# Attention rounds taken in twos on TensorE: scores and maxima of two rounds, then row sums and value products of two rounds

## The chip, the cores and the metric

The kernel runs on one core of a Trainium2 chip. The metric is the device time of one execution in microseconds (us), the median of several runs. The engines named below are TensorE (PE in the rows; PEld is its weight load, which can overlap matmuls), VectorE (DVE), ScalarE (ACT), GpSimd (POOL) and SyncE (SP, which here only issues DMAs).

## What is computed

A layer norm, then attention with ALiBi bias and a causal mask, plus a top-1 mixture of experts on the same normed input. Shapes: x is 2 x 2048 x 512, 16 heads of 32, 8 experts.

```python
xn = layernorm(x)
q, k, v = split(xn @ W_qkv)                       # to heads: (2, 16, 2048, 32)
attn = softmax(q @ k.T / sqrt(32) + alibi + causal_mask)
y = (attn @ v) @ W_o
idx = argmax(softmax(xn @ wg)); gate = max(softmax(xn @ wg))
out = x + y + gate * (xn @ W[idx].T + b[idx])
```

## The kernel before

The program has four parts one after another: projections and routing (`project_and_route`), attention (`attend`), the experts (`run_experts`) and the sum (`combine`). The change is in `attend` alone.

**Groups and rounds.** `attend` works through 8 groups `g` of 4 heads (`HG`). The queries of a group are cut in 4 chunks of 512 (`QC`), the keys in 16 blocks of 128. A round is one chunk and one key block; with the causal mask a chunk `c` needs 4(c+1) blocks, so a group has `NR` = 40 rounds (`ROUNDS`): 4, 8, 12 and 16 in the four chunks. The last 4 rounds of a chunk lie on the diagonal: their tiles are 512, 384, 256 and 128 columns wide and get an extra small matmul that adds the mask (L1129). Group 0 is written out with a plan of its own (`PLAN_FIRST`), groups 1 to 6 use `PLAN_MID` (2 to 5 of them in a hardware loop of two groups per turn), group 7 uses `PLAN_LAST`.

**What TensorE does in a round.** Four scores (`score_unit`, L1126, one per head, full 128-column array, into one of `S_BANKS` = 3 PSUM banks in turn); ScalarE takes the exponential of each bank into `probs` (L1061) and so frees it. Between the scores lie units of the row maxima (`max_unit`, L1091, with a mask matmul L1094 on the diagonal; `M_BANKS` = 3 banks), which VectorE reduces (L975). These maxima belong to rounds far ahead, four units per round in the middle groups (5 to 6 in group 0, none in the last 26 rounds of group 7). Then come the value products of the round before (`value_products`, L1170): four matmuls of 32 columns each, one per head, side by side in the array. The row sums (`row_sums`) have the same 32-column form: on a diagonal round straight from `probs` (L1161); elsewhere two rounds (a pair, `PAIR_OF`) are first added by GpSimd (L959) and TensorE sums the pair (L1137) two rounds later. A matmul of the row sums or value products is shown as two in the trace (x8 for four heads). Below, the 32-column work is called tile work and a run of it a tile block.

**The order.** It is written out by hand: in round r the scores and maxima go unit by unit; the row sums of round r-1 stand in the middle of them (at `hh == HG // 2`, L1191), the value products of round r-1 at the end (L1195).

**The end of a chunk.** Both accumulators lie in one pair of PSUM banks (`acc_ps`). After the last round of a chunk ScalarE copies them out (`leave`, L1043), VectorE inverts the denominators in four quarters (L1010), one each at the end of its next rounds, and GpSimd multiplies (L936); SyncE stores the result (L851). The copy waits until the store of the chunk two before has landed (`y_stored`, L1042), since it overwrites that buffer. `LEAVE_AT`, `INVERT_AT` and `Y_BEFORE_PAIR` say at which round or pair each of these steps stands.

**SyncE's queue** goes in a fixed order: the rows of maxima of later chunks (L842, L846), the load of the next group's queries, keys and values (L813 to L834), which waits for the value products of the group before, and the stores. A store that is issued behind the group's load lands after it. In group 0 the load of group 1 also waits until GpSimd has scattered the normed rows to their expert slots; that scatter stands in GpSimd's queue behind its first additions and the first chunk's multiplication.

Of the kernel before, what the change touches and what calls it, by code (L numbers as in the profile page):

```python
# [26 lines left out]
HG = P // DH  # L27
# [3 lines left out]
QC = S // CH  # L31
# [17 lines left out]
ROUNDS = [(c, jb) for c in range(QC) for jb in range(TPC * (c + 1))]  # L49
NR = len(ROUNDS)  # L50
# [10 lines left out]
NPAIR = len(PAIR_OF) // 2  # L61
PAIR_LAST = {p: r for r, p in PAIR_OF.items()}
LAST_ROUND = [max(r for r, (cc, _) in enumerate(ROUNDS) if cc == c) for c in range(QC)]
# [3 lines left out]
UNIT, FOLD, TURN, SPLIT = "unit", "fold", "turn", "split"  # L67
# [69 lines left out]
def plan_of(g, last):  # L137
# [3 lines left out]
    if isinstance(g, int) and g == 0:  # L141
# [3 lines left out]

LEAVE_AT = {(LAST_ROUND[c] + 1) % NR: ((LAST_ROUND[c] + 1) // NR, c) for c in range(QC)}
QUARTERS = 4
INVERT_AT = {(LAST_ROUND[c] + 2 + k) % NR: ((LAST_ROUND[c] + 2 + k) // NR, c, k)  # L150
             for c in range(QC) for k in range(QUARTERS)}

Y_BEFORE_PAIR = {min([p for p in range(NPAIR) if PAIR_LAST[p] > (LAST_ROUND[c] + 2 + QUARTERS) % NR] or [NPAIR]):
                 ((LAST_ROUND[c] + 2 + QUARTERS) // NR, c) for c in range(QC)}


class Memory:
# [583 lines left out]
def attend(nc, m):  # L741
# [6 lines left out]
    with ExitStack() as c:  # L748
# [24 lines left out]
        max_rows_loaded = [sem("max_rows_loaded0"), sem("max_rows_loaded1")]  # L773
# [11 lines left out]
        MAX_ROWS = 16 * (1 + 2 * HG)  # L785
# [19 lines left out]
        with nc.Block() as block:  # L805
# [268 lines left out]
            def _(pe):  # L1074
# [22 lines left out]
                def maxima(events, banks, g, half, taken):  # L1097

                    for dg, kind, n in events:
                        if (dg, kind, n) == (1, UNIT, 0):  # L1100

                            pe.wait_ge(aug_loaded[1 - half], AUG * ((g + 1) // 2 + 1))
                        if isinstance(g, int) and g == 0 and (dg, kind, n) == (0, UNIT, OF_CHUNK[1][0]):
                            pe.wait_ge(first_loaded[1], AUG)
                        if isinstance(g, int) and g == 0 and (dg, kind, n) == (0, UNIT, OF_CHUNK[QC - 1][0]):

                            pe.wait_ge(aug_loaded[0], AUG)
                        bank, earlier = banks[dg, kind, n]
                        bank_free(earlier, g, taken)
                        if kind == UNIT:  # L1110
                            max_unit((half + dg) % 2, n, bank)
                        else:
                            pe.wait_ge(neg_done, (g + dg) * QC + n + 1)
                            nc.tensor.transpose(max_ps[:, bank, 0:P], neg_max[:], m.ident[:]).then_inc(max_turned, 1)
# [33 lines left out]
                def has_row_sums(r):  # L1148
                    return r not in PAIR_OF or r - 2 in PAIR_LAST.values()

                def row_sums(g, r, exps, adds):

                    cc, jb = ROUNDS[r]
                    off = max(0, jb - TPC * cc) * P
                    probs_of(g, r, exps)

                    if r - 2 in PAIR_LAST.values():
                        pair_product(PAIR_OF[r - 2], ROUNDS[r - 2] == (cc, 1), adds)
                    if r not in PAIR_OF:
                        for hh in range(HG):  # L1160
                            nc.tensor.matmul(den_ps[hh * DH:(hh + 1) * DH, off:CH], m.ones[:],  # L1161
                                             probs[:, r % P_SLOTS, hh, off:CH], start=jb == 0, stop=r == LAST_ROUND[cc])
# [12 lines left out]
                def step(g, half, first, last):  # L1175
                    if first:
                        pe.wait_ge(first_loaded[2], AUG)
                    pe.wait_ge(v_loaded[half], 16 * (g // 2 + 1))
                    exps, adds = base(pe, g, NSU), base(pe, g, NPAIR * HG)
                    taken = base(pe, g, NMU), None if last else base(pe, g + 1, NMU)  # L1180
                    plan, banks = plan_of(g, last)
                    for r in range(NR + 1):
                        events = [e for e in plan[r] if e[1] in (UNIT, TURN)] if r < NR else []
                        if r < NR and ROUNDS[r][1] == 0:

                            cc = ROUNDS[r][0]
                            pe.wait_ge(max_rows_loaded[cc % 2], MAX_ROWS * (g * (QC // 2) + cc // 2 + 1))
                        for hh in range(HG):
                            if r < NR:
                                score_unit(half, r, hh, first, exps)  # L1190
                            if r and hh == HG // 2 and has_row_sums(r - 1):  # L1191
                                row_sums(g, r - 1, exps, adds)
                            maxima(events[len(events) * hh // HG:len(events) * (hh + 1) // HG], banks, g, half, taken)
                        if r:
                            value_products(g, half, r - 1, exps)  # L1195

                pe.wait_ge(first_loaded[0], AUG)
                events = [e for e in PLAN_BEFORE[0] if e[1] in (UNIT, TURN)]
# [317 lines left out]
```

## Time and profile before

| | us |
|---|---|
| median of 3 runs | 1939.15 |
| lowest, highest | 1935.37, 1945.24 |
| span of the profiled execution | 1937.1 |
| TensorE busy | 1789.7 (92%) |
| VectorE busy | 1131.4 (58%) |
| ScalarE busy | 913.7 (47%) |
| GpSimd busy | 665.3 (34%) |
| TensorE, scores L1126, 1280 matmuls | 531.1 |
| TensorE, maxima L1091, 1280 matmuls | 523.6 |
| TensorE, value products L1170, 2560 matmuls | 308.6 |

The span runs from the first to the last instruction; the median of the runs is 2.05 us above it. Attention takes the time from about 340 to 1668 us. The last group's copy of its last chunk begins at 1667.9; those of groups 0 to 6 at 592.5, 750.5, 906.4, 1071.1, 1225.2, 1381.3 and 1539.3. In a table of windows each engine has its busy time, and PEclk is the granted TensorE clock as a share of full speed (1.00 is 2.4 GHz, 0.50 is 1.2 GHz).

### The profile page before, as it was taken

The numbers are of one execution on the slowest core, as the hardware profiler recorded it, in microseconds if no ns is written. First come the engines' busy times: TensorE is split into PE (matmuls) and PEld (weight loads), VectorE is DVE, ScalarE is ACT, GpSimd is POOL, SyncE is SP. The second block draws the span as 40 slices with busy tenths as digits, with TensorE's granted clock in tenths as the row PEclk, the third lists the DMA queues.
The fourth block names the chain that finished last, engine by engine and source line by source line (L and its number), as shares of the span: only waits on it lengthen the run. The fifth ranks groups of instructions, "written<-read, shape, count | busy, mean of one in ns | idle before, by whom it ended". The sixth has DMA issues, their size and how long they took to land. (4 is left out here: it accounts for less than half of the span.)

```text
span 1937.1 us, 31890 instructions
## 1 busy us (share of the span) xinstructions
PE 1789.7 (92%) x10482; PEld 1023.6 (53%) x10483; DVE 1131.4 (58%) x2001; ACT 913.7 (47%) x1575; POOL 665.3 (34%) x665
## 2 busy tenths in 40 slices
PE   5999999589699999999999999999999999789798
PEld 4777777344344444444444444444444443478687
DVE  5433334577487577666665667767766670344366
ACT  3222222055356566565565566656656567621211
POOL 6000000067152452442444246245244346211260
PEclk9999999588899899999899899999989999899999
DMA  6667744959508205502700900730450230244496
GB/s 229 220 216 261 266 168 147 163 204 252 64 7 145 32 7 104 68 14 58 114 8 9 169 8 7 139 39 7 99 72 8 76 116 12 104 152 163 145 390 240
DMA packets 102350, 227.81 MB, mean 118 GB/s; under 512 B 9832, under 2 KB 27240, under 8 KB 96648
## 3 DMA queue, kind: packets, MB, share of 16 engines
q1 hardware_dynamic: 87648, 176.20, 36.3%
q0 software_dynamic: 14560, 49.75, 7.0%
q8 instruction: 84, 1.38, 0.3%
q14 instruction: 58, 0.48, 0.1%
HBM read 128.47 MB, written 96.93 MB: 116 GB/s over the span
## 5 line engine op out<-in xcount | busy, mean ns | idle before, releaser
L1061 ACT ACTIVATE probs_sb<-score_ps,bias 128x512 f32<-128x512 f32 (+3 forms) x1280 | 733.1, 624 | 506.2 <-PE score_ps L1129 303.7
L975 DVE TENSOR_REDUCE part_max<-max_ps 128x1 f32<-128x512 f32 (+3 forms) x1280 | 722.0, 603 | 394.5 <-PE max_ps L1091 203.0
L959 POOL TENSOR_TENSOR pair_sum<-probs_sb 128x512 f32<-128x512 f32 x384 | 479.8, 1281 | 592.5 <-ACT probs_sb L1061 592.3
L1126 PE MATMUL score_ps<-q_aug,k_aug 100*128 100x512 f32 (+3 forms) x1280 | 531.1, 422 | 42.3 <-ACT probs_sb L1061 24.4
L1091 PE MATMUL max_ps<-k_aug,q_aug 98*128 98x512 f32 (+3 forms) x1280 | 523.6, 421 | 40.1 <-DMA q_aug<-q_rows_d 33.4
L1126 PEld LDWEIGHTS score_ps<-q_aug,k_aug 100*128 100x128 f32 x1280 | 251.3, 197 | 305.9 <-ACT probs_sb L1061 231.5
L1091 PEld LDWEIGHTS max_ps<-k_aug,q_aug 98*128 98x128 f32 x1280 | 260.2, 204 | 181.7 <-DVE part_max L975 104.7
L1170 PE MATMUL acc_ps<-probs_sb,v_sb 128*32 128x512 f32 (+3 forms) x2560 | 308.6, 555 | 0.0
L1010 DVE RECIPROCAL acc_sb<-acc_sb 128x128 f32<-128x128 f32 x128 | 119.6, 939 | 74.0 <-ACT acc_sb L1043 74.0
L618 DVE SCALAR_TENSOR_TENSOR st_lo<-group_ps,st_hi 128x512 fp32r<-128x512 f32 x64 | 44.3, 692 | 139.1 <-ACT st_hi L665 138.4
L1094 PE MATMUL max_ps<-mask_qk,ident_bf 128*128 128x128 bf16 x512 | 124.3, 243 | 0.0
L1129 PE MATMUL score_ps<-mask_kq,ident_bf 128*128 128x128 bf16 x512 | 120.0, 235 | 0.0
L665 ACT ACTIVATE st_hi<-group_ps 128x512 fp32r<-128x512 f32 x64 | 38.3, 598 | 143.0 <-PE group_ps L728 124.2
L728 PE MATMUL group_ps<-xT_hi,w_hi 128*128 128x512 f32 x256 | 102.7, 401 | 0.0
L1137 PE MATMUL acc_ps<-pair_sum,ones 128*32 128x512 f32 x768 | 102.3, 605 | 0.0
L728 PE MATMUL group_ps<-xT_lo,w_hi 128*128 128x512 f32 x256 | 101.9, 398 | 0.0
L728 PE MATMUL group_ps<-xT_hi,w_lo 128*128 128x512 f32 x256 | 101.7, 397 | 0.0
L1161 PE MATMUL acc_ps<-probs_sb,ones 128*32 128x512 f32 (+3 forms) x1024 | 97.3, 452 | 1.2 <-ACT acc_sb L1043 1.2
L1094 PEld LDWEIGHTS max_ps<-mask_qk,ident_bf 128*128 128x128 bf16 x512 | 52.7, 103 | 75.1 <-issue 56.9
L1129 PEld LDWEIGHTS score_ps<-mask_kq,ident_bf 128*128 128x128 bf16 x512 | 50.6, 99 | 69.1 <-issue 48.6
L1170 PEld LDWEIGHTS acc_ps<-probs_sb,v_sb 128*32 128x32 f32 x2560 | 51.5, 109 | 63.7 <-issue 39.8
L466 POOL DMA_DIRECT2D slot_x_d<-zero_f x20 | 14.2, 715 | 172.2 <-PE group_ps L728 172.2
(177 smaller groups left out, 1684.5 us busy)
## 6 DMA issues: line engine op xcount, KB each, us to landing
k_aug<-k_hi_d SPq DMA_DIRECT2D x14, 1024.0 KB
q_aug<-q_hi_d SPq DMA_DIRECT2D x14, 1024.0 KB
slot_x_d<-zero_f POOLq DMA_DIRECT2D x20, 512.0 KB, 7.1
rows<-slot_x_d SPq DMA_DIRECT2D x40, 256.0 KB, 2.6
slot_y_d<-y_rows POOLq DMA_DIRECT2D x39, 256.0 KB, 2.5
xn_d<-xn SPq DMA_DIRECT2D x8, 1024.0 KB, 9.9
q_hi_d<-st_hi SPq DMA_DIRECT2D x32, 256.0 KB, 7.7
q_lo_d<-st_lo SPq DMA_DIRECT2D x32, 256.0 KB, 7.6
```

The costliest lines, as they stand in the source:

```text
L728: last = nc.tensor.matmul(group_ps[:, n % BANKS], lhs, rhs, start=(k == 0 and p == 0), stop=(k == KC - 1 and p == 2))
L959: nc.gpsimd.tensor_tensor(pair_sum[:, p % 2, hh], probs[:, s0, hh], probs[:, s1, hh], ALU.add).then_inc(pair_added, 1)
L975: nc.vector.tensor_reduce(part_max[:, hh * QT + i, kc:kc + 1], max_ps[:, bank, 0:w], AX.X, ALU.max).then_inc(max_taken, 1)
L1010: nc.vector.reciprocal(quarter, quarter).then_inc(inverted, 1)
L1061: nc.scalar.activation(probs[:, r % P_SLOTS, hh, off:CH], score_ps[:, (r * HG + hh) % S_BANKS, off:CH], ACT.Exp, bias=bias[:, half, hh * Q ...
L1091: last = nc.tensor.matmul(max_ps[:, bank, 0:w], q_aug[0:ROW_MAX, half, hh, i * P:(i + 1) * P], k_aug[0:ROW_MAX, half, hh, kc * CH:kc * CH ...
L1094: last = nc.tensor.matmul(max_ps[:, bank, w - P:w], m.ident_bf[:], m.mask_qk[:], start=False, stop=True)
L1126: last = nc.tensor.matmul(score_ps[:, u % S_BANKS, off:CH], k_aug[0:ROWS, half, hh, jb * P:(jb + 1) * P], q_aug[0:ROWS, half, hh, cc * CH ...
L1129: last = nc.tensor.matmul(score_ps[:, u % S_BANKS, off:off + P], m.ident_bf[:], m.mask_kq[:], start=False, stop=True)
L1137: last = nc.tensor.matmul(den_ps[hh * DH:(hh + 1) * DH, :], m.ones[:], pair_sum[:, p % 2, hh], start=start, stop=False)
L1161: nc.tensor.matmul(den_ps[hh * DH:(hh + 1) * DH, off:CH], m.ones[:], probs[:, r % P_SLOTS, hh, off:CH], start=jb == 0, stop=r == LAST_ROUN ...
L1170: last = nc.tensor.matmul(y_ps[hh * DH:(hh + 1) * DH, off:CH], v_sb[:, half, jb, hh * DH:(hh + 1) * DH], probs[:, r % P_SLOTS, hh, off:CH] ...
```

## The change

The loop over rounds becomes a loop over pairs of rounds (r0, r0+1). For each, TensorE runs the eight scores and their maxima in a row, then the row sums and value products of the two rounds r0-2 and r0-1. Nothing is added to or taken from the matmuls. As the value products of a chunk's last round now come one round later, the copy, the reciprocals and the multiplication are moved one round later too.

```diff
-LEAVE_AT = {(LAST_ROUND[c] + 1) % NR: ((LAST_ROUND[c] + 1) // NR, c) for c in range(QC)}
+LEAVE_AT = {(LAST_ROUND[c] + 2) % NR: ((LAST_ROUND[c] + 2) // NR, c) for c in range(QC)}
 QUARTERS = 4
-INVERT_AT = {(LAST_ROUND[c] + 2 + k) % NR: ((LAST_ROUND[c] + 2 + k) // NR, c, k)
+INVERT_AT = {(LAST_ROUND[c] + 3 + k) % NR: ((LAST_ROUND[c] + 3 + k) // NR, c, k)
              for c in range(QC) for k in range(QUARTERS)}
...
-                    for r in range(NR + 1):
-                        events = [e for e in plan[r] if e[1] in (UNIT, TURN)] if r < NR else []
...
-                        for hh in range(HG):
-                            if r < NR:
+                    for r0 in range(0, NR + 2, 2):
+                        for r in (r0, r0 + 1) if r0 < NR else ():
+                            events = [e for e in plan[r] if e[1] in (UNIT, TURN)]
...
+                            for hh in range(HG):
                                 score_unit(half, r, hh, first, exps)
-                            if r and hh == HG // 2 and has_row_sums(r - 1):
-                                row_sums(g, r - 1, exps, adds)
-                            maxima(events[len(events) * hh // HG:len(events) * (hh + 1) // HG], banks, g, half, taken)
-                        if r:
-                            value_products(g, half, r - 1, exps)
+                                maxima(events[len(events) * hh // HG:len(events) * (hh + 1) // HG], banks, g, half, taken)
+                        for r in (r0 - 2, r0 - 1) if r0 else ():
+                            if has_row_sums(r):
+                                row_sums(g, r, exps, adds)
+                            value_products(g, half, r, exps)
```

`Y_BEFORE_PAIR` changes in the same way (+2 to +3), and gives the same pairs as before.

TensorE in the fourth chunk of group 1, a pair of full-width rounds. Before, one round with the pair's row sums in its middle:

```order
L1126 MATMUL score_ps<-q_aug,k_aug 128x512
L1091 MATMUL max_ps<-k_aug,q_aug 128x128
L1094 MATMUL max_ps<-mask_qk,ident_bf 128x128
L1126 MATMUL score_ps<-q_aug,k_aug 128x512
L1137 MATMUL acc_ps<-pair_sum,ones 32x512 x4
L1091 MATMUL max_ps<-k_aug,q_aug 128x128
L1094 MATMUL max_ps<-mask_qk,ident_bf 128x128
L1126 MATMUL score_ps<-q_aug,k_aug 128x512
L1091 MATMUL max_ps<-k_aug,q_aug 128x128
L1094 MATMUL max_ps<-mask_qk,ident_bf 128x128
L1170 MATMUL acc_ps<-probs_sb,v_sb 32x512 x4
L1126 MATMUL score_ps<-q_aug,k_aug 128x512
```

The change, the end of one pair's units and the start of the next:

```order
L1126 MATMUL score_ps<-q_aug,k_aug 128x512
L1091 MATMUL max_ps<-k_aug,q_aug 128x256
L1094 MATMUL max_ps<-mask_qk,ident_bf 128x128
L1170 MATMUL acc_ps<-probs_sb,v_sb 32x512 x4
L1137 MATMUL acc_ps<-pair_sum,ones 32x512 x4
L1170 MATMUL acc_ps<-probs_sb,v_sb 32x512 x4
L1126 MATMUL score_ps<-q_aug,k_aug 128x512
L1091 MATMUL max_ps<-k_aug,q_aug 128x512
```

Three separate tile blocks in a pair of rounds have become one.

TensorE in the last group, where no maxima are left. Before:

```order
L1126 MATMUL score_ps<-q_aug,k_aug 128x512 x3
L1137 MATMUL acc_ps<-pair_sum,ones 32x512 x4
L1126 MATMUL score_ps<-q_aug,k_aug 128x512
L1170 MATMUL acc_ps<-probs_sb,v_sb 32x512 x4
L1126 MATMUL score_ps<-q_aug,k_aug 128x512 x4
L1170 MATMUL acc_ps<-probs_sb,v_sb 32x512 x4
```

The change:

```order
L1126 MATMUL score_ps<-q_aug,k_aug 128x512 x8
L1170 MATMUL acc_ps<-probs_sb,v_sb 32x512 x4
L1137 MATMUL acc_ps<-pair_sum,ones 32x512 x4
L1170 MATMUL acc_ps<-probs_sb,v_sb 32x512 x4
L1126 MATMUL score_ps<-q_aug,k_aug 128x512 x8
```

Eight scores now follow each other with nothing between them, against three banks.

ScalarE in a middle group at the passage from the second chunk to the third, with the semaphores that each instruction waits for (`scored`: TensorE's score; `pv_done`: the value products; `y_stored1`: the store two chunks back). Before:

```order
L1061 ACTIVATE probs_sb<-score_ps,bias 128x512 [waits scored,pv_done]
L1061 ACTIVATE probs_sb<-score_ps,bias 128x512 [waits scored] x3
L1043 ACTIVATE acc_sb<-acc_ps 128x1024 [waits y_stored1,pv_done]
L1061 ACTIVATE probs_sb<-score_ps,bias 128x512 [waits scored,pv_done]
L1061 ACTIVATE probs_sb<-score_ps,bias 128x512 [waits scored] x3
```

The change:

```order
L1061 ACTIVATE probs_sb<-score_ps,bias 128x512 [waits scored,pv_done]
L1061 ACTIVATE probs_sb<-score_ps,bias 128x512 [waits scored] x3
L1061 ACTIVATE probs_sb<-score_ps,bias 128x512 [waits scored,pv_done]
L1061 ACTIVATE probs_sb<-score_ps,bias 128x512 [waits scored] x3
L1043 ACTIVATE acc_sb<-acc_ps 128x1024 [waits y_stored1,pv_done]
L1061 ACTIVATE probs_sb<-score_ps,bias 128x512 [waits scored,pv_done]
```

The copy stands one round of four exponentials later.

## Rows read from the trace of the kernel before

**Rows 1.** Windows of middle and last groups: length, busy per engine, PEclk, DMA share, GB/s.

```profile
1100.00:1300.00 200.00, 194.04 (x1289) 90.00 (x1285) 138.01 (x245) 123.61 (x217) 85.72 (x70) 0.98 0.32 53
1600.00:1700.00 100.00, 82.31 (x568) 39.62 (x561) 26.37 (x40) 67.09 (x122) 42.81 (x36) 0.94 0.15 56
```

**Rows 2.** Timeline, TensorE, middle group: start, us, engine, line, operation, count.

```profile
704.18 0.50 PE L1126 MATMUL score_ps<-q_aug,k_aug 100*128 100x512 f32 x1
...
709.94 0.40 PE L1126 MATMUL score_ps<-q_aug,k_aug 100*128 100x512 f32 x1
...
710.17 0.39 PE L1091 MATMUL max_ps<-k_aug,q_aug 98*128 98x512 f32 x1
...
710.49 1.06 PE L1170 MATMUL acc_ps<-probs_sb,v_sb 128*32 128x512 f32 x8
...
711.49 0.50 PE L1126 MATMUL score_ps<-q_aug,k_aug 100*128 100x512 f32 x1
...
711.82 0.28 PE L1091 MATMUL max_ps<-k_aug,q_aug 98*128 98x256 f32 x1
...
740.37 1.07 PE L1137 MATMUL acc_ps<-pair_sum,ones 128*32 128x512 f32 x8
741.25 0.83 PE L1161 MATMUL acc_ps<-probs_sb,ones 128*32 128x384 f32 x8
```

**Rows 3.** Timeline, ScalarE and VectorE in the same group; then page row of the reciprocals.

```profile
704.80 2.42 ACT L1061 ACTIVATE probs_sb<-score_ps,bias 128x512 f32<-128x512 f32 x4 [0.96 <-PE score_ps L1126]
...
719.56 2.48 DVE L975 TENSOR_REDUCE part_max<-max_ps 128x1 f32<-128x512 f32 x4 [0.83 <-PE max_ps L1091]
...
L1010 DVE RECIPROCAL acc_sb<-acc_sb 128x128 f32<-128x128 f32 x128 | 119.6, 939 | 74.0 <-ACT acc_sb L1043 74.0
```

**Rows 4.** Last group: timeline of ScalarE and TensorE, then a window, TensorE alone.

```profile
1621.80 2.45 ACT L1061 ACTIVATE probs_sb<-score_ps,bias 128x512 f32<-128x512 f32 x4
...
1622.57 0.50 PE L1126 MATMUL score_ps<-q_aug,k_aug 100*128 100x512 f32 x1 [0.99 <-ACT probs_sb L1061]
1622.99 1.06 PE L1170 MATMUL acc_ps<-probs_sb,v_sb 128*32 128x512 f32 x8
...
1629.51 0.96 PE L1126 MATMUL score_ps<-q_aug,k_aug 100*128 100x512 f32 x3
...
1635.60 0.96 PE L1126 MATMUL score_ps<-q_aug,k_aug 100*128 100x512 f32 x3
...
1640.00:1650.00 10.00, 9.05 (x53) 1.00 0.07 27
```

**Rows 5.** Load, store, copy of a middle group: timeline, a window, waits, then group 4.

```profile
744.05 0.64 SPq L842 DMA_DIRECT2D q_aug<-q_rows_d  x1
...
750.02 0.36 SPq L813 DMA_DIRECT2D k_aug<-k_hi_d  x1
...
747.56 0.47 PE L1126 MATMUL score_ps<-q_aug,k_aug 100*128 100x512 f32 x1
...
797.88 1.02 ACT L1043 ACTIVATE acc_sb<-acc_ps 128x1024 f32<-128x1024 f32 x1 [3.45 <-DMA y_d<-acc_sb]
...
799.54 0.80 PE L1126 MATMUL score_ps<-q_aug,k_aug 100*128 100x512 f32 x1 [3.33 <-ACT probs_sb L1061]
...
800.00:805.00 5.00, 5.00 (x21) 2.20 (x21) 2.74 (x6) 2.61 (x6) 4.52 (x4) 0.54 0.00 0
...
ACT acc_sb L1043 <- DMA y_d<-acc_sb: 19.0, 5, 4.1
...
1065.25 0.38 SPq L813 DMA_DIRECT2D k_aug<-k_hi_d  x1
...
1066.25 0.76 PE L1126 MATMUL score_ps<-q_aug,k_aug 100*128 100x512 f32 x1 [4.43 <-DMA q_aug<-max_lo]
```

**Rows 6.** Group 0: GpSimd's first multiplication; what TensorE waited for, 470 to 510.

```profile
432.32 1.28 POOL L936 TENSOR_TENSOR acc_sb<-acc_sb 128x512 f32<-128x512 f32 x1 [0.18 <-DVE acc_sb L1010]
...
PE max_ps L1091 <- DMA q_aug<-q_rows_d: 15.6, 1, 15.6
```

More of the change, by code:

```diff
@@ L143, in plan_of @@
     return PLAN_MID, BANKS_MID
-LEAVE_AT = {(LAST_ROUND[c] + 1) % NR: ((LAST_ROUND[c] + 1) // NR, c) for c in range(QC)}
+LEAVE_AT = {(LAST_ROUND[c] + 2) % NR: ((LAST_ROUND[c] + 2) // NR, c) for c in range(QC)}
 QUARTERS = 4
-INVERT_AT = {(LAST_ROUND[c] + 2 + k) % NR: ((LAST_ROUND[c] + 2 + k) // NR, c, k)
+INVERT_AT = {(LAST_ROUND[c] + 3 + k) % NR: ((LAST_ROUND[c] + 3 + k) // NR, c, k)
              for c in range(QC) for k in range(QUARTERS)}
-Y_BEFORE_PAIR = {min([p for p in range(NPAIR) if PAIR_LAST[p] > (LAST_ROUND[c] + 2 + QUARTERS) % NR] or [NPAIR]):
-                 ((LAST_ROUND[c] + 2 + QUARTERS) // NR, c) for c in range(QC)}
+Y_BEFORE_PAIR = {min([p for p in range(NPAIR) if PAIR_LAST[p] > (LAST_ROUND[c] + 3 + QUARTERS) % NR] or [NPAIR]):
+                 ((LAST_ROUND[c] + 3 + QUARTERS) // NR, c) for c in range(QC)}
 class Memory:
@@ L1181, in step @@
                     plan, banks = plan_of(g, last)
-                    for r in range(NR + 1):
-                        events = [e for e in plan[r] if e[1] in (UNIT, TURN)] if r < NR else []
-                        if r < NR and ROUNDS[r][1] == 0:
-                            cc = ROUNDS[r][0]
-                            pe.wait_ge(max_rows_loaded[cc % 2], MAX_ROWS * (g * (QC // 2) + cc // 2 + 1))
-                        for hh in range(HG):
-                            if r < NR:
-                                score_unit(half, r, hh, first, exps)
-                            if r and hh == HG // 2 and has_row_sums(r - 1):
-                                row_sums(g, r - 1, exps, adds)
-                            maxima(events[len(events) * hh // HG:len(events) * (hh + 1) // HG], banks, g, half, taken)
-                        if r:
-                            value_products(g, half, r - 1, exps)
+                    for r0 in range(0, NR + 2, 2):
+                        for r in (r0, r0 + 1) if r0 < NR else ():
+                            events = [e for e in plan[r] if e[1] in (UNIT, TURN)]
+                            if ROUNDS[r][1] == 0:
+                                cc = ROUNDS[r][0]
+                                pe.wait_ge(max_rows_loaded[cc % 2], MAX_ROWS * (g * (QC // 2) + cc // 2 + 1))
+                            for hh in range(HG):
+                                score_unit(half, r, hh, first, exps)
+                                maxima(events[len(events) * hh // HG:len(events) * (hh + 1) // HG], banks, g, half, taken)
[3 more added lines that the diff above has]
+                            value_products(g, half, r, exps)
                 pe.wait_ge(first_loaded[0], AUG)
```

## The prediction, made before the changed kernel was run

> **What bounds the kernel now.** I read the windows first, to see which engine is full in which stage. In the middle groups TensorE is busy 194 of 200 us, VectorE 138 and ScalarE 124; in the last group TensorE is busy 82 of 100 us and ScalarE 67 [rows 1]. So seven of eight groups go by TensorE's queue, and the last one by TensorE and ScalarE in turn. A busy share near full says nothing of waste inside it, so the timeline of TensorE came next, read by start times: what a matmul costs is the distance to the next start. Then the waits, for what holds TensorE up at all: in each of five middle groups ScalarE's copy waits for a store, 19.0 us together, and in group 0 TensorE waits 15.6 us once for a load [rows 5, 6].
>
> **What the change removes: switches between full matmuls and tile blocks.** In a steady run the next full matmul starts after 0.23 us (709.94 to 710.17). Before a tile block it takes 0.32 (to 710.49): 0.09 more. A 512-wide block of four heads takes 0.88 us if tile work follows it (740.37 to 741.25), but 1.00 if a full matmul does (710.49 to 711.49): 0.12 more. The first full matmul behind it takes 0.33 instead of 0.23, since its weight load is not hidden: 0.10 more [rows 2]. One tile block between full matmuls so costs 0.09 + 0.12 + 0.10 = 0.31 us of switching. (The Trainium skill, TensorEngine Tiling (Array Packing), section Key Properties, says that a change of tiling mode drains the engine; it gives no price, and the rows agree with 0.31 us.)
>
> How many go: before, a group has 39 blocks at ends of rounds (the last holds rounds 38 and 39) and 24 in the middle of rounds (15 diagonal rounds, and 9 of the 12 pair sums; the other three stand beside diagonal ones). That is 63. After, there are 20 pairs, the last two tile blocks touch, so 19. 44 fewer x 0.31 = **13.6 us per group**, 109 us over eight groups. That is the gross gain, and I do not expect most of it to arrive.
>
> **What it adds: eight units in a row against three banks.** ScalarE takes the first exponential 0.62 us after the first score starts (704.18 to 704.80) and four take 2.42 us, so about 0.58 each [rows 2, 3]. A score may start 0.77 us after the start of the exponential that empties its bank (1621.80 to 1622.57) [rows 4]. The eighth score needs the fifth exponential: 0.62 + 4 x 0.58 + 0.77 = 3.71 us after the first. TensorE itself would be there after 0.33 + 0.23 + 6 x 0.46 = 3.3 to 3.4. So it waits about 0.35, and a held matmul shows its weight load (0.10), which makes 0.45 us per full-width pair. Before, a tile block after at most four scores gave ScalarE that time for nothing. A middle group has 12 such pairs: 5.4 us. In the 8 diagonal pairs the scores are narrower, and VectorE paces instead: four reductions in 2.48 us, 0.60 each, hardly below 3.9 us for the eighth maximum where TensorE's narrower units would need 3.2 to 3.6. I take 0.4 each, 3.2 us. Then the reciprocals, 0.94 us each [rows 3]: before, there was one per round, worked off during the tile blocks. Now 8 of the 20 pairs hold two, the first one between the fourth and the fifth maximum of a run that VectorE already paces, and in four of these ScalarE starts with its copy (1.02 us) [rows 5]. Of the 0.94 I take 0.4 to 0.5 as visible, with the turn of the maxima in the middle of a run: 3.5 us net of what such places cost now. Sum **+12.1 us per middle group**, so nets to -1.5 us, or -9 us for six. The unknown here is the pace: with 0.15 us per pair less or more it is 18 us either way in these six groups, 23 in all.
>
> Nothing else lengthens in between: GpSimd's four additions of a pair (5 us of a 7 us pair) now wait until the sums of two pairs ago are used, some 2 us later than now, and their results are wanted two pairs on. Registers and semaphores are the same in number. I cost these at nothing; the cover is the idle half of GpSimd.
>
> **What it moves: the store that arrives late.** In five middle groups ScalarE waits 3.45 to 4.1 us (19.0 in all) at the copy of the second chunk; TensorE then stands still for 3.3 us, and after that runs at about half clock for some 5 us (0.54 from 800 to 805), 2.3 to 2.7 us lost [rows 5]. A place so costs about 6.3 us, five are 31.5. The store lands 47.9 us after SyncE starts to issue the next group's load (750.02 to 797.88), because it lies behind that load; the load itself starts 2.5 us after the group's first score (747.56), because SyncE is still issuing rows of maxima from 744.05 on, for about 5.6 us. So it lands at 50.3 us of the group. After the change the turn of those maxima has the second half of a run of eight and the tile work of four rounds between it and the group's end, over 7 us in place of 4.7, so the load starts with the group and the store lands at about 48. The copy comes one round of scores later: before, the value products of round 11 were through at 46.7; less 15 switches (4.7 us), plus round 13's units (1.9) and about 5 us of the new waits, they end at 48 to 49. So the wait goes or nearly so, and with it the drop of the clock. Group 4 supports this: there the load started 1.0 us before the first score (1065.25, 1066.25), and its copy did not wait [rows 5]. I take **-31.5 us**; if only the timing of the load were unchanged, it would be 0 to -10.
>
> **Group 0.** Its first part is bound by GpSimd's queue: the multiplication of chunk 0 follows the last reciprocal with hardly a wait (0.18 us), and behind it stand the rest of the scatter, the load of group 1 and TensorE's wait of 15.6 us for it [rows 6]. The last reciprocal now comes a round later, behind 5 or 6 more reductions (3.3 us and the turn): +4 us, straight to the end of that wait. What TensorE itself loses before it is absorbed by the 15.6. Behind the load 19 rounds with 5.6 maxima each follow, where VectorE needs 11 x 0.60 + reciprocals per pair and stood closest to the limit: +0.5 us per pair, 5 us. Together **+9 us**.
>
> **The last group.** Its first 14 rounds are as in a middle group, 0. Then no maxima stand between the scores: a pair takes 3.71 to the eighth score, 0.42 from a held score to the tile block (1622.57 to 1622.99), and 0.88 + 0.88 + 1.00 of tile work: 6.89 us, against 6.09 now (1629.51 to 1635.60) [rows 2, 4]. Nine full pairs at +0.8 and four diagonal ones at about +0.5: **+9 us**.
>
> **Sum.** -9 - 31.5 + 9 + 9 = -22.5 us on the span of 1937.1, which gives 1914.6; with the 2.05 us between that span and the median, **1917 us**.
>
> **The rivals.**
> 1. The pace hides: VectorE and ScalarE start each run empty, and if the waits come to about 0.2 us per pair instead of 0.45, some 36 us more stay: 1917 - 36 = 1881. For it: both are a third or more idle in the middle groups. Against: 3.71 is a chain of measured distances.
> 2. The late store stays late. If the load of the next group starts no sooner after the first score, the copy meets the same 50.3 us, and rounds that go faster only wait longer: the 31.5 us are not gained, 1948. It decides at the first 12 rounds: the value products of round 11 have to end after the store lands, with a margin of a few tenths by my sum.
> 3. Slower by the pace: a bank's hand-over costs more when two engines hold TensorE in turns, because each held matmul shows its load. At 0.2 us more per pair, 156 pairs give +31: 1948; at 0.3, 1964. For it speaks the last group, which waits for ScalarE at nearly each round already. This is slower from +0.08 us per pair on top of mine being wrong elsewhere, or from +0.2 alone.
> 4. The clock. Now TensorE waits some tenths in many rounds of the last group, and the granted clock stays at 1.00 [rows 4]; it falls only behind waits of 3 us and more. A wait in each run that did lower it, say one half-clock stretch of 2.3 us per chunk, would give 32 x 2.3 = +74: 1991. (The Trainium skill, TensorE: Matmul & The Clock Gate, section A second HAM failure mode: psum-queue depth-cycling, tells of a kernel that cycles through PSUM banks and whose short idle times between groups of matmuls make the clock swing. The trace disagrees so far as waits of some tenths go.)
> 5. That the change does not do what it says can be left out: the order of instructions shows the merged blocks.
>
> **Chances.** Mine 0.50, with a range of its own of 1900 to 1932; rival 1 0.16; rival 2 0.14; rival 3 0.16; rival 4 0.03; 0.01 for the rest. For 8 in 10, the range leaves out half of rival 1's far side and rival 4 with the far half of rival 3: 1885 to 1953. About 0.5% (9.7 us) is what a measurement can tell from no change: faster means below 1929.5, slower above 1948.8. Faster: 0.44 of mine and rival 1, 0.60; same: the rest of mine and half of rivals 2 and 3, 0.19; slower 0.21.
>
> **What would show it.** Right: 19 tile blocks per group, pairs of about 7.0 to 7.1 us in the fourth chunk of the middle groups instead of 7.3 (704.18 to 711.49), no wait of the copy at L1043 for a store, no clock below 0.9 behind it, a last group some 9 us longer than its 128.6, and a copy of group 0's last chunk some 9 us later. Wrong: pairs of 6.7 us (rival 1), a wait of 3 us or more at L1043 with the half-clock stretch behind it (rival 2), pairs of 7.3 or more (rival 3), PEclk under 0.9 all through a group (rival 4).

## The result: 2.7% faster, more than twice the gain that was forecast

The changed kernel takes **1890.15 us** (median of 4 runs, 1886.1 to 1890.46) against 1937.34 for the kernel before, measured beside it: a ratio of 0.973 (95% interval 0.971 to 0.976), 47 us less. The forecast was 1917 with a range of 1885 to 1953: the direction was right and the time lies in the range, but the likeliest case forecast 22 us less (1939.15 to 1917), and its own range of 1900 to 1932 was missed. The largest term that failed is the pace, +12.1 us per middle group. The profiled execution spans 1884.5 us against 1937.1.

The account by groups comes from ScalarE's copy of each group's last chunk (L1043 in ScalarE's timeline). After the change it begins at 603.75, 748.30, 892.73, 1045.10, 1193.26, 1337.59, 1481.93 and 1614.46 us.

| | before | after | difference | forecast |
|---|---|---|---|---|
| start to group 0's last copy | 592.5 | 603.8 | +11.3 | +9 |
| groups 1 to 6 | 946.8 | 878.2 | -68.6 | -40.5 |
| group 7 | 128.6 | 132.5 | +3.9 | +9 |
| to the end of the span | 269.2 | 270.0 | +0.8 | 0 |
| span | 1937.1 | 1884.5 | -52.6 | -22.5 |

So the question of this study is the 28 us in the middle groups. In every kernel below group 3 takes 5 to 9 us more than its undisturbed neighbours 1, 2, 5 and 6. Between groups 3 and 4 the hardware loop turns; TensorE stands still there for 4.4 us in the changed kernel and then runs at a granted clock of 0.50 from 1036 to 1056 us. An order can be compared best in the undisturbed groups; the expectations give their length as that of the middle groups (151.0, 144.35), the results below give the mean of all six.

The window of the profile of after that answers to the first of [rows 1] (length, then busy time of TensorE, its weight load, VectorE, ScalarE and GpSimd, then PEclk, DMA share, GB/s):

```profile
1100.00:1300.00 200.00, 196.88 (x1375) 103.30 (x1377) 145.00 (x264) 128.88 (x235) 94.27 (x77) 1.00 0.26 47
```

TensorE is as full as before and does 1375 matmul records in the time of 1289; its clock is 1.00 instead of 0.98. A busy share would have shown nothing of the gain.

TensorE's timeline in the fourth chunk of group 5, the end of one pair and of the next, to be held against [rows 2]:

```profile
1291.28 1.07 PE L1170 MATMUL acc_ps<-probs_sb,v_sb 128*32 128x512 f32 x8
1292.16 1.04 PE L1137 MATMUL acc_ps<-pair_sum,ones 128*32 128x512 f32 x8
1293.02 1.04 PE L1170 MATMUL acc_ps<-probs_sb,v_sb 128*32 128x512 f32 x8
...
1298.19 1.07 PE L1170 MATMUL acc_ps<-probs_sb,v_sb 128*32 128x512 f32 x8
```

Tile work next to tile work takes 0.88 and 0.86 to the next start, and a pair 6.91 us here (6.91 to 7.06, mean 6.98) against 7.31.

ScalarE's timeline at the copies that waited for a store in [rows 5], in groups 1 and 2, then the sums of the waits of that copy (us in total, times, longest):

```profile
647.37 1.02 ACT L1043 ACTIVATE acc_sb<-acc_ps 128x1024 f32<-128x1024 f32 x1 [0.83 <-DMA y_d<-acc_sb]
...
792.05 1.02 ACT L1043 ACTIVATE acc_sb<-acc_ps 128x1024 f32<-128x1024 f32 x1 [0.94 <-DMA y_d<-acc_sb]
...
ACT acc_sb L1043 <- DMA y_d<-acc_sb: 1.8, 2, 0.9
```

19.0 us of waits have become 1.8. SyncE's queue and TensorE around group 2's beginning show why (SPq is SyncE's issuing):

```profile
743.42 0.51 PE L1126 MATMUL score_ps<-q_aug,k_aug 100*128 100x512 f32 x1
...
743.71 0.36 SPq L813 DMA_DIRECT2D k_aug<-k_hi_d  x1
```

The load starts 0.3 us after the group's first score, where it was 2.5, and the copy that waited for the store's landing starts 48.6 us after that score (792.05 - 743.42).

### The profile page after: what moved, and what is told of

Read it like the earlier page. It is cut to its first block and busy times, and to the rows that moved or that the text cites. A ratio compares the mean times of both kernels' runs of the same rounds, so it can differ in the third digit from the quotient of the medians.

```text
span 1884.5 us, 31890 instructions
## 1 busy us (share of the span) xinstructions
PE 1736.2 (92%) x10482; PEld 1061.8 (56%) x10483; DVE 1109.1 (59%) x2001; ACT 884.4 (47%) x1575; POOL 665.2 (35%) x665
## 5 line engine op out<-in xcount | busy, mean ns | idle before, releaser
L1061 ACT ACTIVATE probs_sb<-score_ps,bias 128x512 f32<-128x512 f32 (+3 forms) x1280 | 706.3, 630 | 479.0 <-PE score_ps L1129 223.4
L975 DVE TENSOR_REDUCE part_max<-max_ps 128x1 f32<-128x512 f32 (+3 forms) x1280 | 700.1, 600 | 356.0 <-PE max_ps L1091 267.8
L1091 PE MATMUL max_ps<-k_aug,q_aug 98*128 98x512 f32 (+3 forms) x1280 | 533.7, 427 | 50.7 <-DMA q_aug<-q_rows_d 36.2
L1170 PE MATMUL acc_ps<-probs_sb,v_sb 128*32 128x512 f32 (+3 forms) x2560 | 293.9, 538 | 0.0
L1170 PEld LDWEIGHTS acc_ps<-probs_sb,v_sb 128*32 128x32 f32 x2560 | 73.3, 110 | 113.8 <-issue 95.4
```

Source lines behind the costliest of these rows:

```text
L975: nc.vector.tensor_reduce(part_max[:, hh * QT + i, kc:kc + 1], max_ps[:, bank, 0:w], AX.X, ALU.max).then_inc(max_taken, 1)
L1061: nc.scalar.activation(probs[:, r % P_SLOTS, hh, off:CH], score_ps[:, (r * HG + hh) % S_BANKS, off:CH], ACT.Exp, bias=bias[:, half, hh * Q ...
L1091: last = nc.tensor.matmul(max_ps[:, bank, 0:w], q_aug[0:ROW_MAX, half, hh, i * P:(i + 1) * P], k_aug[0:ROW_MAX, half, hh, kc * CH:kc * CH ...
L1170: last = nc.tensor.matmul(y_ps[hh * DH:(hh + 1) * DH, off:CH], v_sb[:, half, jb, hh * DH:(hh + 1) * DH], probs[:, r % P_SLOTS, hh, off:CH] ...
```

## The experiments

Each edit is made in the kernel before or in the changed one; ratios are against the kernel before, run beside them on the same chip (1939.7, 1939.6 and 1940.5 us in the three sets). "Middle groups" is the sum of groups 1 to 6 over six, from the copies of one profiled execution. The same order on TensorE in groups 1 to 6 gave 146.4, 146.3 and, with two short stretches of half clock, 147.3 (the changed kernel, e6, e4).

### The late store by itself

In the kernel before, and later in others, GpSimd issues the store right behind its multiplication, in a queue with no load in it:

```diff
-                    sp.wait_ge(y_done, g * QC + cc + 1)
-                    sp.dma_start(m.y_d[g, :, cc * CH:(cc + 1) * CH], y_sb[:, cc % 2]).then_inc(y_stored[cc % 2], 16)
+                    pool.wait_ge(y_done, n + 1)
+                    pool.dma_start(m.y_d[g, :, cc * CH:(cc + 1) * CH], y_sb[:, cc % 2]).then_inc(y_stored[cc % 2], 16)
```

> The kernel before, with the attention output stored by GpSimd right behind its multiplication, not by SyncE behind the next group's load. The order on TensorE is untouched. If the late store and the clock behind it cost 6.3 us in five places: -31 us. If only the wait itself counts, and the clock would have fallen elsewhere: -17 us. If the store then lands as late as now: no change.

Measured (e3): 1911.07 us, ratio 0.986 (0.983 to 0.989). No copy waits for a store; middle groups fall from 157.8 to 152.4 us, **32.6 us** in all six. The forecast's term was 31.5. The median falls by less, 28.6: group 0 ends 1.8 us later and the part behind attention takes 3.6 us more (1.9 to 5.2 in e6, e9 and e7 against the same kernels with SyncE's store); why, was not followed.

> The changed kernel with the attention output stored by GpSimd. Its copy waited for a store only twice, 1.8 us in all. If the late store is the gain's main part in the changed kernel, there is nothing left to win: within 3 us of 1890. With the third experiment (1911) this gives the changed order alone, without the late store: 1911 - 1889 = 22 us, or 6.7 us in each middle group less what groups 0 and 7 lose, where the prediction had 1.5.

Measured (e6): 1894.16 us, 0.977 (0.974 to 0.980), middle groups 146.3 as in the changed kernel (146.4). There was nothing left to win in these groups. The median is 4 us above the changed kernel's, outside the 3 that were expected, and 3.3 of them are in the last group. So the late place explains 32.6 of the 68.6 us, and the order the other **36 us, 6.0 per group, where the forecast had 1.5**. The kernels that follow take that difference apart.

### Switches without twos

The kernel before, with the row sums moved out of the middle of a round:

```diff
-                            if r and hh == HG // 2 and has_row_sums(r - 1):
-                                row_sums(g, r - 1, exps, adds)
...
                         if r:
+                            if has_row_sums(r - 1):
+                                row_sums(g, r - 1, exps, adds)
                             value_products(g, half, r - 1, exps)
```

> The kernel before, with the row sums of round r-1 moved from the middle of round r's scores to just ahead of its value products. 24 of 63 tile blocks per group go (39 are left), a run of scores stays at four, and no table is changed. If a block costs 0.31 us of switching: 192 x 0.31 = 60 us off in all, less what the late store takes back (the second chunk's copy waits longer by what the first 12 rounds gain, some 3 us in five groups): about -45 us. If a block costs 0.40 us, as the changed kernel's extra gain would ask for: -60 us. If grouping is worth little by itself and the changed kernel's gain is the late store's alone: under -15 us.

Measured (e1): 1916.85 us, 0.989 (0.987 to 0.992). A full pair falls from 7.31 to 6.98 us, 0.33 for one block: the price of 0.31 holds there. But the median fell by 23 us where the price times 192 blocks had given 45. The copy still waits for the store, 22.8 us in five places: the faster rounds only meet it earlier, as rival 2 said. And the blocks pay in the middle groups alone: group 0 ends 3.5 us later than before and the last group takes 3.1 us more.

> The kernel before with two edits: the row sums stand beside the value products (24 tile blocks fewer, as in the run that had this edit alone), and GpSimd issues the store of the result, so that no copy waits for it. Between the kernel before with that store (1911, middle groups 151.0 us) and the changed kernel's tables with single rounds and that store (1876, middle groups 143.0 to 143.5) it stands one edit from each: it prices the 24 blocks without the store's wait, and then the distance of two. Theory A (the switch price carries the gain, 0.23 us for an average block by the clean chunks): middle groups 145.4, median about 1911 - 8 x 5.6 = 1867 to 1875 since group 0 stays early, so near 1872. Theory B (the distance of two itself gives more than 2 us per group, and the clean chunks flattered this edit): middle groups 147 or more, median above 1880.

Measured (e9): 1877.61 us, 0.966 (0.963 to 0.969). Middle groups 146.7: with the store out of the way the 24 blocks give **5.7 us per group** (0.24 each on average; 7.4 at the full price). Theory A was right in the undisturbed groups (145.1 to 145.5 against 145.4); the median lies 6 us above its 1872. Group 0 ends 3.1 us later than in e3, so it does not stay early, and the last group takes 0.5 more. This one edit and the store, at distance one, beat the whole change.

### The distance of two

The changed kernel's tables, but rounds one by one:

```diff
+                    for r in range(NR + 2):
+                        if r < NR: ...
+                        if r >= 2:
+                            if has_row_sums(r - 2):
+                                row_sums(g, r - 2, exps, adds)
+                            value_products(g, half, r - 2, exps)
```

> The changed kernel's tables and its distance of two rounds between scores and products, but one round at a time: scores and maxima of round r, then sums and products of round r-2. 39 tile blocks per group instead of 19, runs of four units instead of eight. If runs of eight cost 0.45 us per pair of waits and a block 0.31 us, this is about level with the changed kernel (20 blocks x 0.31 = 6.2 us more, 20 pairs x 0.45 = 9 us less per group: 1870). If the pace costs only 0.2 us per pair: 1905 us.

Measured (e2): 1885.0 us, 0.972 (0.969 to 0.976). With 38 blocks per group (the last two touch; the expectation counted 39) where the changed kernel has 19 it is at least as fast. Its middle groups take 147.3 us, since the copy still waits for the store, 8.0 us in five places.

> One round at a time at a distance of two rounds, with GpSimd's store. The copy still waited 8.0 us in five groups in the second experiment, and its group without a wait took 143.3 us against 144.3 of the changed kernel. If twos are worth nothing beside the distance: 1885 - 8 - some clock = 1874 to 1878, below the sixth experiment by over 10 us. If the twos help once the store is out of the way: equal to it or above.

Measured (e7): 1876.19 us, 0.967 (0.964 to 0.969); middle groups 145.1. From the run before this in the chain (e9) that is -1.6 us per group; from here to the twos with the same store (e6) it is **+1.2 per group**. The last group takes 126.6 us, against 132.5 to 135.8 in twos. (With the same order in the last group, e8 takes 129.2: its clock is at 0.50 from 1552 to 1556 us.)

All but 0.3 of the -1.6 was in no term of the forecast. TensorE's runs between tile blocks show most of it at one place, the start of the fourth chunk. VectorE, GpSimd and TensorE there in the kernel before (L982 and L987 are the turn of a chunk's maxima, L1114 its transpose on TensorE):

```profile
1321.67 5.00 POOL L959 TENSOR_TENSOR pair_sum<-probs_sb 128x512 f32<-128x512 f32 x4 [18.63 <-ACT probs_sb L1061]
...
1323.09 0.94 DVE L1010 RECIPROCAL acc_sb<-acc_sb 128x128 f32<-128x128 f32 x1
...
1324.26 1.21 DVE L987 TENSOR_TENSOR neg_max<-max_shift,row_max 128x16 f32<-128x16 f32 x1 [0.18 <-DVE row_max L982]
...
1326.13 0.50 PE L1091 MATMUL max_ps<-k_aug,q_aug 98*128 98x512 f32 x1 [0.85 <-DVE part_max L975]
...
1326.80 0.32 PE L1114 MATMUL max_ps<-ident,neg_max 128*128 128x128 f32 x1 [0.17 <-DVE part_max L975]
1327.05 1.06 PE L1170 MATMUL acc_ps<-probs_sb,v_sb 128*32 128x512 f32 x8
```

A reciprocal (0.94) stands ahead of the turn, and the turn's small subtraction takes 1.21 us. Behind it the reductions are late and TensorE is held: the run from 1323.37 to 1327.05 takes 3.68 us where its neighbours take 2.07. With the tables one round later the turn comes ahead of the first reciprocal. The changed kernel, same place:

```profile
1279.97 0.18 DVE L987 TENSOR_TENSOR neg_max<-max_shift,row_max 128x16 f32<-128x16 f32 x1 [0.18 <-DVE row_max L982]
...
1283.02 0.94 DVE L1010 RECIPROCAL acc_sb<-acc_sb 128x128 f32<-128x128 f32 x1
```

TensorE at distance two with single rounds (e7; L1115 is the transpose of the turn there), the same run:

```profile
1274.80 0.50 PE L1127 MATMUL score_ps<-q_aug,k_aug 100*128 100x512 f32 x1
...
1277.25 0.27 PE L1115 MATMUL max_ps<-ident,neg_max 128*128 128x128 f32 x1
1277.45 1.07 PE L1171 MATMUL acc_ps<-probs_sb,v_sb 128*32 128x512 f32 x8
```

It takes 2.65 us (2.57 to 2.79 in the six middle groups), where it took 3.67 to 3.69 in e9 and before: 1.0 less, half of the 1.9 to 2.1 us by which the fourth chunk is shorter from copy to copy.

The tables without the distance (the row sums beside the products, distance one, later copy and reciprocals):

> The first experiment's kernel (row sums beside the value products, distance of one round) with the changed kernel's three tables: copy, reciprocals and multiplication one round later. If the late store is met by the later copy alone, the wait of 4.2 to 4.8 us in five groups shrinks by about a round (3 us) and with it the drop of the clock: -20 us against the first experiment, near 1897. If the distance of two rounds itself is what helps, it stays within 5 us of 1917.

Measured (e5): 1926.53 us, 0.992 (0.989 to 0.994), neither of the two expected values, and slower than e1. No copy waits for a store any more, but (in the trace of its longest execution, 1939.95 us):

```profile
PE acc_ps L1170 <- ACT acc_sb L1043: 34.8, 24, 2.2
```

The value products of a new chunk now wait for the copy of the old one, 24 times. So the later copy alone cures the wait for the store and puts another in its place: the later tables need the later value products, and the distance is what lets them be late.

### What a run of eight costs

One PSUM bank is moved from the maxima to the scores, in the changed kernel with GpSimd's store:

```diff
-S_BANKS, M_BANKS, P_SLOTS = 3, 3, 4
+S_BANKS, M_BANKS, P_SLOTS = 4, 2, 4
```

> The changed kernel with GpSimd's store (1894, middle groups 144.35 us, last group 132 to 136) and four PSUM banks for the scores and two for the maxima, in place of three and three. If what a run of eight still costs (0.29 us per pair against single rounds) is ScalarE's hand-over of score banks, as the prediction's chain has it, the eighth score needs the fourth exponential and not the fifth: up to 0.58 us less. The last group, with no maxima in its last 26 rounds, then goes from 132.5 to about 127 to 128 (ten full pairs at 6.4 to 6.5 in place of 6.82). In middle groups it also shows whether VectorE paces: with two banks for the maxima each has to be read within one unit more. Theory A (VectorE has slack, as the missing 5 us of the forecast suggest): middle groups 144 or less. Theory B (VectorE is close to the limit in diagonal pairs): middle groups 147 or more, since a reduction takes 0.60 us and two hand-overs stand in a row.

Measured (e10): 1993.96 us, 1.027 (1.023 to 1.03), 100 us slower than with three and three. In the last group, where no maxima are left, the bank does what the chain of distances says. TensorE, three banks of scores (the changed kernel):

```profile
1579.02 0.97 PE L1126 MATMUL score_ps<-q_aug,k_aug 100*128 100x512 f32 x3
...
1583.12 1.07 PE L1170 MATMUL acc_ps<-probs_sb,v_sb 128*32 128x512 f32 x8
```

and four:

```profile
1694.33 1.19 PE L1127 MATMUL score_ps<-q_aug,k_aug 100*128 100x512 f32 x4
...
1697.85 1.07 PE L1171 MATMUL acc_ps<-probs_sb,v_sb 128*32 128x512 f32 x8
```

From the first score to the tile block 4.10 against 3.52 us: 0.58, one exponential. The last group as a whole went from 135.8 to 131.5, not to the 127 or 128 expected, since its first 14 rounds carry maxima. In the middle groups the full pairs of the fourth chunk have runs of 4.71 to 5.12 us in place of 4.20 to 4.35, and a group is 14.7 us longer. Theory B was right: with two banks VectorE holds TensorE inside a run, though with three it is busy only 145 of 200 us, and the third bank hides most of that.

Then the reciprocals, which the forecast had charged with most of 3.5 us per group. They invert 8 columns in place of 128, in both kernels (with GpSimd's store); the other denominators stay uninverted:

```diff
-                    nc.vector.reciprocal(quarter, quarter).then_inc(inverted, 1)
+                    nc.vector.reciprocal(quarter[:, 0:8], quarter[:, 0:8]).then_inc(inverted, 1)
```

> The kernel before with GpSimd's store (1911, middle groups 151.0 us), in which each reciprocal of the denominators inverts 8 columns in place of 128, so that it takes some 0.1 us of VectorE in place of 0.94 (15 us less VectorE per group). The rest of the denominators stays as it is, so the output's attention part is not the reference's. If a reciprocal of the kernel before was in nobody's way, as the prediction has it (worked off during the tile blocks), the middle groups stay at 151.0 within 0.5. If some of it was on TensorE's path before, they fall by up to 16 x 0.4 = 6 us. Group 0 ends some 4 to 8 us earlier in either case, since the multiplication of its first chunk follows the last reciprocal.

> The same edit (8 columns in place of 128 in each reciprocal, the rest of the denominators as it is) in the changed kernel with GpSimd's store (1894, middle groups 144.35 us). The prediction charged about 3.5 us per middle group for reciprocals, copy and turn that meet a run of eight. If that is there and is the reciprocals', the middle groups fall to about 141 and the step from the kernel before to it widens by as much. If the charge was wrong, they stay at 144 within 0.5, as before.

Measured (e11 and e12): 1897.52 us (0.977, 0.974 to 0.980) and 1871.86 us (0.963, 0.960 to 0.966). Middle groups 150.4 and 143.7, so the reciprocals cost 2.0 us per group before and 2.6 after. In neither kernel were they free, and what the change adds to them is **0.6 us**, not some 3. Before, their cost stands in the two runs with the turn: with short reciprocals the one in the fourth chunk takes 2.42 to 2.45 us in place of 3.67 to 3.69, the one in the third 1.96 to 2.02 in place of 2.85 to 2.88, together 2.1 us. Group 0 did not get shorter, against the expectation (595.5 and 607.1 to its last copy, 594.2 and 605.7 without the edit); why, was not followed.

### The last group and group 0

In the changed kernel, group 7 alone one round at a time (`if last:` takes the loop with single rounds above):

> The changed kernel, but the last group takes one round at a time at a distance of two (39 blocks, runs of four scores), groups 0 to 6 as in the changed kernel. If runs of eight scores against ScalarE cost 0.6 us per full pair there and 20 blocks cost 6 us: nine full pairs give -5 us and the diagonal ones nothing, so -3 to -6 us against the changed kernel; if the pace costs nothing there, +5 us.

Measured (e4): 1885.08 us, 0.972 (0.970 to 0.974). The last group falls from 132.5 to 126.6 us, also below the 128.6 of before. There the twos cost 5.9 us, 1.1 of them by the clock (two tile blocks at about half clock take 2.93 in place of 1.85 us).

In the kernel at distance two with single rounds and GpSimd's store, group 0 alone at distance one with the tables of before:

```diff
+                    lag = 1 if first else 2
...
-                        if r >= 2:
+                        if r >= lag:
```

> As the seventh, but group 0 at a distance of one round with the tables of the kernel before (copy and reciprocals one round earlier). Group 0 ended 9 to 11 us later in the changed kernel and the second experiment and 3.5 us later in the first. If the later last reciprocal of chunk 0 on GpSimd's queue is the cause: 4 to 8 us below the seventh. If the merging of the sums is the cause: level with it.

Measured (e8): **1872.46 us, 0.965 (0.963 to 0.968)**, the fastest of all, 67 us below the kernel before and 18 below the changed one; it computes the same as both. That is 3.7 below e7, where 4 to 8 were expected. Group 0's last copy comes 5.0 us earlier (604.7 to 599.8); the last group, whose order is that of e7, takes 2.6 us more in a stretch of half clock. GpSimd's first multiplication in the changed kernel, to be held against the first of [rows 6], and in this one:

```profile
438.16 1.28 POOL L936 TENSOR_TENSOR acc_sb<-acc_sb 128x512 f32<-128x512 f32 x1 [5.45 <-DVE acc_sb L1010]
```

```profile
435.79 1.26 POOL L939 TENSOR_TENSOR acc_sb<-acc_sb 128x512 f32<-128x512 f32 x1
```

## Why the prediction was right in direction and short by half

**Right, and shown.** The price of a switch, 0.31 us: one block less takes 0.33 off a full pair (7.31 to 6.98). The late place at the second chunk: 31.5 forecast, 32.6 when it alone is removed; the load starts with the group, the copy at 48.6 us of the group where 48 to 49 was worked out, the wait and the half clock behind it are gone. Rival 2 did not come, though by little: two copies still waited 0.8 and 0.9 us, in e4 with the same order in these groups two waited 1.2 and 1.7, and the 22.8 us of waits in the run with the row sums alone show what it would have been. That a margin of some tenths held was in part luck. Group 0: +11.3 against +9; GpSimd's multiplication comes 5.8 us later, behind a wait of 5.45 for the reciprocal, and giving group 0 its old distance takes 5.0 us back. Of the other 5 or 6 us the forecast put 5 behind the load; 3.1 to 3.5 of them are there already when the row sums alone are moved (e9 against e3, e1 against the kernel before), 2.1 of these at GpSimd's first multiplication, which is ahead of the load. So the number came out partly for another reason. Rival 4 came only on a small scale: waits of 0.2 to 0.9 us in the middle groups leave the granted clock at 1.00 in the window above. (The rule of the Trainium skill, TensorE: Matmul & The Clock Gate, section A second HAM failure mode: psum-queue depth-cycling, does not describe these groups.) Yet the clock does not fall behind waits of 3 us and more alone, as the forecast had it: in the last group, after a run in which TensorE waits 0.82 us once for ScalarE, the stretch from 1568 to 1570 us is at 0.52 and the next at 0.63. Such stretches of 2 to 6 us stand in single rounds too (e8), in middle groups of e4 and e6, and differ between kernels with the same order, so they blur the comparison of last groups by 1 to 3 us.

**Wrong: the pace term, 12.1 us per middle group.** Between kernels that have no late store the order gives 6.0 us per group, where 13.6 - 12.1 = 1.5 was forecast. By the chain of kernels:

| step | measured per group | forecast |
|---|---|---|
| 24 blocks in mid-round (e3 to e9) | -5.7 | -7.4 |
| distance of two, later tables, one block (e9 to e7) | -1.6 | -0.3 |
| 19 blocks fewer, runs of eight (e7 to e6) | +1.2 | -5.9 + 12.1 |
| sum | -6.0 | -1.5 |

The forecast of the first line was 1.7 too high, and if the 9 blocks in full pairs gave 0.33 each, the other 15, in diagonal rounds, gave 0.18 each. The second line is 1.3 beyond its block: most of it shows as the run of 3.68 us at the start of the fourth chunk, of which the late tables take 1.0 away; the forecast had looked only for what the change puts in a worse place, not for what stands badly now.

The third line is most of it: if the 19 blocks are worth their full 5.9, the runs of eight cost 7.1 and not 12.1. In that 12.1, three parts. The full pairs: in the fourth chunk, two runs and two blocks of single rounds (2.07 + 1.00 + 2.06 + 1.85 = 6.98) against one run and one block (4.28 + 2.71 = 6.99): the switches saved and the wait are equal, so the wait is 0.31 to 0.33, not 0.45; 12 pairs, 3.9 us, 1.5 less. The reciprocals, the copy and the turn: 3.5 was charged. Against the kernel before, the reciprocals measured by themselves add 0.6: they cost 2.6 now and 2.0 then. The charge took each reciprocal in a run as half visible and those before as free: what changes is the difference. But more than half of those 2.0 had gone with the late tables, in the second line. In e7 the two runs with the turn are on average 0.7 and 0.2 us longer than with short reciprocals in the kernel before, so about 0.9 is left there, and the runs of eight bring back some 1.7 (an estimate from these rows; e7 with short reciprocals was not run). What is left of the 7.1, some 1.5 us, falls to diagonal pairs, copy and turn together (3.2 was charged to the first alone); it is a remainder, not a measurement, and how it divides stays open.

So rival 1 was nearer than my own case. It said 0.2 instead of 0.45 per pair because VectorE and ScalarE start each run empty; whether that had a part was not tested. The hand-over in the last group came as measured off the trace (0.58 per bank), and VectorE's hand-over binds as soon as a bank is taken away. So the step that failed is the size of the pace term, in all its parts (7.1 for 12.1), and beside it a gain was missing: the later tables free the turn (1.3).

**The last group** was forecast at +9 and came at +3.9: nine pairs of 6.82 us against 6.89 forecast, but their like before took 6.09 to 6.38, and I had taken the lowest, 6.09, for all. That explains a part; nine pairs still give more than the 3.9, so the four diagonal pairs, charged at +0.5 each, must have gained something, which was not followed. The twos still lose there: +5.9 against single rounds.

**The twos themselves.** What the change is named after gave nothing: at equal distance and with GpSimd's store single rounds are faster by 1.2 us per middle group (143.0 to 143.5 against 144.3 to 144.4 in the undisturbed ones, one with a stretch of half clock left out), and 18 in the median (1876.19 and 1894.16), of which 9 are in the last group and some 3 of those the clock's. With SyncE's store the two orders come out nearly alike (medians 1885.0 and 1890.15, middle groups 147.3 against 146.4 and 147.3), because the single rounds reach the copy earlier and wait there for the store. The gain came from what came along with it: row sums beside value products, a distance of two, and a load that leaves on time.

## What to carry to other kernels

Put work of one tiling mode side by side, but stop when the runs that this makes are longer than the banks can carry: here one block less per full pair of rounds paid 0.33 us, and a run of eight gave its saving back. When a step is moved, charge it with the difference between its new place and its old one, measured by shortening it in both, and look for what stands badly now. Where a store shares a queue with a large load, try the other queue first: one moved line gave 28.6 us of the 47.

## What the runs showed of the hardware that was not expected

A subtraction of 16 columns on VectorE (L987, both operands in SBUF) takes 0.17 to 0.20 us when nothing holds it, and up to 1.35 in the kernel before. There 17 of its 32 executions take over 0.3 us, and each of these ends 0.03 to 0.04 us after an instruction of GpSimd ends. In the rows of the kernel before at the start of the fourth chunk, GpSimd's four additions start at 1321.67 and take 1.25 each, so the third ends at 1325.42; the subtraction that began at 1324.26 ends at 1325.47. In the changed kernel another, at 1250.63 in additions that began at 1250.45, ends at 1251.76, where the first addition ends at 1251.70:

```profile
1250.45 5.00 POOL L959 TENSOR_TENSOR pair_sum<-probs_sb 128x512 f32<-128x512 f32 x4 [4.58 <-PE acc_ps L1137]
...
1250.63 1.13 DVE L987 TENSOR_TENSOR neg_max<-max_shift,row_max 128x16 f32<-128x16 f32 x1 [0.18 <-DVE row_max L982]
```

It waits for the addition that is running. (The Trainium skill, SBUF — State Buffer, section SBUF: two separate sides, says that a VectorE operation with two SBUF inputs and a GpSimd operation that reads SBUF hold a shared pair of ports in turn, each for a whole instruction; the four ends above agree.) Reductions of 512 columns out of PSUM, most of VectorE's work here, are not held: they take 0.68 us each (0.60 from start to start) beside the same additions and away from them.

And a third PSUM bank for the maxima is worth more than a fourth for the scores, though the two engines have almost equal work per unit (0.60 and 0.58 us): moved from VectorE to ScalarE, the bank gave 0.58 us per pair where no maxima are left, and where both are at work the group took 14.7 us more.
